# A gated delta rule kernel: state update over 128 rows, output products moved behind it, half-width masked copies, one gate projection for two heads

## What is computed

```
tri = tril(einsum('bhncd', k_beta, k) * decay, -1)
Tm = solve_triangular(eye + tri, eye)            # inverse of a 64x64 unit triangle per chunk
v_new = Tm @ v_beta ; k_cum = Tm @ (k_beta * exp(g))
def step(S, inp):                                # from chunk to chunk
    v_n = v_i - kc_i @ S
    out = (q_i * exp(g_i)) @ S + attn @ v_n
    S = S * exp(g_last) + (k_i * exp(g_last - g_i)).T @ v_n
```

## Time and profile before

| | |
|---|---|
| median of 3 runs | 3196.33 us (3190.98 to 3197.37) |
| the profiled execution | 3194.53 us, span 3192.8 us |
| granted TensorE clock, mean | 0.965 |
| TensorE busy | 2971.4 us, 93% of the span |
| VectorE busy | 2307.4 us, 72% |
| ScalarE, GpSimd busy | 1235.1 us, 1020.7 us |
| stage with the change | about 1000 to 2957 us of the span |

### The profile page before, as it was taken

One profiled execution on the slowest core, in us unless ns is written; L12 is line 12 of the kernel. 1 busy time (PEld: TensorE's weight loads), 2 busy tenths in 40 slices (PEclk: granted clock), 3 DMA queues, 4 the chain that ended last, 5 costly groups with the idle time before them and its releaser, 6 DMA issues. The chain is left out here.

```text
span 3192.8 us, 82005 instructions
## 1 busy us (share of the span) xinstructions
PE 2971.4 (93%) x33019; PEld 2051.3 (64%) x33019; DVE 2307.4 (72%) x5231; ACT 1235.1 (39%) x2975; POOL 1020.7 (32%) x1495
## 2 busy tenths in 40 slices
PE   6999999679997999999999999999999999999897
PEld 3444444246663777777777777777777777777565
DVE  4666677878874788688678678678678678676566
ACT  2433333323334344344344344344344344342354
POOL 3555455527772222222222222132132132121011
PEclk8999999789997999999999999999999999998899
DMA  2121111000001111001001001001001001000000
GB/s 83 36 58 31 32 31 34 22 1 1 1 1 47 32 41 32 22 19 32 22 18 32 21 19 32 19 21 32 19 21 32 19 22 32 18 18 2 4 25 27
DMA packets 94040, 80.43 MB, mean 25 GB/s; under 512 B 54992, under 2 KB 68320, under 8 KB 93664
## 3 DMA queue, kind: packets, MB, share of 16 engines
q1 hardware_dynamic: 93664, 75.18, 8.7%
HBM read 57.70 MB, written 4.85 MB: 20 GB/s over the span
## 5 line engine op out<-in xcount | busy, mean ns | idle before, releaser
L1828 PE MATMUL gd_bk<-gd_xT,gd_wh 128*128 128x512 f32 x768 | 397.3, 627 | 8.9 <-DVE gd_KE L1555 7.4
L480 DVE TENSOR_REDUCE at_nm<-at_ring 128x2 f32<-128x256 f32 (+3 forms) x256 | 199.2, 821 | 142.9 <-PE at_ring L623 142.9
L1537 DVE SCALAR_TENSOR_TENSOR gd_YK<-gd_bk,gd_cw,gd_YK 128x511 f32<-128x511 f32 (+2 forms) x384 | 283.1, 743 | 11.8 <-ACT gd_YK L1406 6.1
L1506 ACT COPY gd_ZS<-gd_bk 128x256 f32<-128x256 f32 x320 | 119.1, 372 | 318.3 <-PE gd_bk L2008 312.3
L2008 PE MATMUL gd_bk<-gd_L,gd_NT 64*64 64x64 f32 x5120 | 203.7, 223 | 26.5 <-DVE gd_L L1597 25.9
L2008 PEld LDWEIGHTS gd_bk<-gd_L,gd_NT 64*64 64x64 f32 x5120 | 169.2, 134 | 78.8 <-DVE gd_L L1597 40.2
L1595 DVE COPY_PREDICATED gd_U<-gd_mU,gd_bk 128x256 f32<-128x256 int32 x320 | 141.0, 442 | 105.5 <-PE gd_bk L2030 75.1
L1493 ACT COPY gd_O<-gd_bk 64x128 f32<-64x128 f32 x448 | 108.5, 259 | 274.8 <-PE gd_bk L1966 273.9
L2025 PE MATMUL gd_bk<-gd_U,gd_ZS 64*64 64x64 f32 x5120 | 207.6, 220 | 0.1
L302 POOL TENSOR_TENSOR at_PT<-at_PT,at_dm 128x1024 f32<-128x1024 f32 (+3 forms) x128 | 197.8, 1545 | 10.6
L2025 PEld LDWEIGHTS gd_bk<-gd_U,gd_ZS 64*64 64x64 f32 x5120 | 174.6, 135 | 40.8 <-issue 37.1
(11 more groups left out here) (354 smaller groups left out, 6772.0 us busy)
## 6 DMA issues: line engine op xcount, KB each, us to landing
gd_wh<-in_L_attn_W_qkvz SPq DMA_DIRECT2D x64, 512.0 KB, 3.7
gd_gb<-gates SPq DMA_DIRECT2D x128, 64.0 KB, 3.3
X<-in_L_attn_x SPq DMA_DIRECT2D x8, 512.0 KB, 8.7
at_QT<-at_QS SPq DMA_DIRECT2D x128, 32.0 KB, 2.0
at_KT<-at_KS SPq DMA_DIRECT2D x128, 32.0 KB, 2.0
at_OC<-at_Ob SPq DMA_DIRECT2D x128, 32.0 KB, 2.0
at_RC<-inverse SPq DMA_DIRECT2D x128, 32.0 KB, 1.8
out_x<-X SPq DMA_DIRECT2D x8, 512.0 KB, 2.9
```

The costliest lines, as they stand in the source:

```text
L480: nc.vector.tensor_reduce(nm[v % 2][:, k, c0:c0 + HS + 1:HS], set_of(s, 2 + p)[:, :, 0:n], AX.X, ALU.max).then_inc(max_done, 1)
L1537: nc.vector.scalar_tensor_tensor(out[:, s:W], bank_[:, 0:W - s], cw[:, j, head(f, e), CONVK - 1 - s:CONVK - s], out[:, s:W], ALU.mult, ALU ...
L1828: ins = nc.tensor.matmul(out[:, :], wh[e][:, k, col * DK:(col + 1) * DK], xT[:, k, :], start=k == 0, stop=k == DC - 1)
```

## The change

Four edits, all in `delta_rule`:

1. The state update of the rounds 1 to 7 contracts over all 128 rows. `V2` becomes a tile with one 128-row copy per chunk in which the other chunk's 64 rows are zero (cleared once by 4 memsets), and KK is read over all rows. The update of round 0 still has 64 rows.
2. TensorE computes the output products (odd rounds) directly behind the state update, ahead of the late piece of the next pair. Behind the levels the new values of both heads come first, then the new keys of both.
3. The masked copies of the levels 1 to 5 touch only the 32 of each 64 columns that the mask can select. Source, mask and destination are read in runs of 2, 4, 8, 16 or 32 columns. The masks are built 256 wide. The level 0 copies keep their width.
4. The gate projection computes both heads at once: 2 matmuls of 256 columns for each of 4 row tiles in place of 4 of 128. The weights of both heads lie in one tile and come by one DMA, which waits for the queries of both heads.

```diff
-        mU = [sb(f"mU{l}", [P, CK], I32) for l in range(LEVELS)]
+        mU = [sb(f"mU{l}", [P, TPS, CK], I32) for l in range(LEVELS)]
...
+        def side(tile, l, bit):
+            return tile[:, :, :].rearrange("p t (b s n) -> p (t b) s n", s=2, n=1 << l)[:, :, bit, :]
...
+        def bank_side(b_, half, l, bit):
+            return b_[:, half * TPS * CK:(half + 1) * TPS * CK].rearrange("p (b s n) -> p b s n", s=2, n=1 << l)[:, :, bit, :]
...
-        V2, O = [sb(f"V2{e}", [P, TPS, DK]) for e in E2], [sb(f"O{e}", [P, TPS, DK]) for e in E2]
+        V2, O = [sb(f"V2{e}", [P, 2, CPT, DK]) for e in E2], [sb(f"O{e}", [P, TPS, DK]) for e in E2]
...
                 def level(f, e, l):
                     dve.wait_ge(y_mm[e], f * (LEVELS - 1) + l)
-                    last = nc.vector.copy_predicated(U[e][:, :, :], wide(mU[l]), chunks(A_[e], 1))
+                    last = nc.vector.copy_predicated(side(U[e], l, 1), side(mU[l], l, 1), bank_side(A_[e], 1, l, 1))
                     if l < LEVELS - 1:
-                        last = nc.vector.copy_predicated(L[e][:, :, :], wide(mL[l]), chunks(A_[e], 0))
+                        last = nc.vector.copy_predicated(side(L[e], l, 0), side(mL[l], l, 0), bank_side(A_[e], 0, l, 0))
...
-                def gate_in(f, e, i):
-                    ge(pe, kc_done[e], f)
-                    for t in (2 * i, 2 * i + 1):
-                        for k in range(DC):
-                            last = nc.tensor.matmul(F1[e][:, t * P:(t + 1) * P], xT[:, k, t * P:(t + 1) * P], wh[e][:, k, 3 * DK:4 * DK],
-                                                    start=k == 0, stop=k == DC - 1)
-                    if i == 1:
-                        last.then_inc(zp_mm[e], 1)
+                def gate_in(f, t):
+                    i = t // 2
+                    ge(pe, kc_done[i], f)
+                    for k in range(DC):
+                        last = nc.tensor.matmul(F1[i][:, t % 2 * 2 * DK:(t % 2 + 1) * 2 * DK].rearrange("p (e n) -> p e n", e=2),
+                                                xT[:, k, t * P:(t + 1) * P], wh[:, k, :, 3 * DK:4 * DK], start=k == 0, stop=k == DC - 1)
+                    if t % 2 == 1:
+                        last.then_inc(zp_mm[i], 1)
...
-                                    moving = V2[e][rows(c), t, :]
-                                nc.tensor.matmul(A_[e][:, DK:2 * DK], KK[e][q % 2][rows(c), t, :], moving, start=True, stop=True).then_inc(ds_mm[e], 1)
-                        if has(f):
-                            front_late(f, n)
+                                    fixed, moving = KK[e][q % 2][:, t, :], V2[e][:, t % 2, c, :]
+                                nc.tensor.matmul(A_[e][:, DK:2 * DK], fixed, moving, start=True, stop=True).then_inc(ds_mm[e], 1)
...
                                 last.then_inc(oi_mm[e], 1)
+                        if has(f):
+                            front_late(f, n)
...
                             last.then_inc(vk_mm[e], 1)
+                        for e in E2:
                             pe.wait_ge(at_done[e], f + 1)
```

More of the change, by code:

```diff
@@ L971, in delta_rule @@
         m1, m2 = sb("m1", [P, CK], I32), sb("m2", [P, CK], I32)
-        mU = [sb(f"mU{l}", [P, CK], I32) for l in range(LEVELS)]
-        mL = [sb(f"mL{l}", [P, CK], I32) for l in range(LEVELS - 1)]
+        mU = [sb(f"mU{l}", [P, TPS, CK], I32) for l in range(LEVELS)]
+        mL = [sb(f"mL{l}", [P, TPS, CK], I32) for l in range(LEVELS - 1)]
         xT = sb("xT", [P, DC, W])
@@ L1175, in delta_rule @@
         kT, vT = [sb(f"kT{e}", [P, W]) for e in E2], [sb(f"vT{e}", [P, W]) for e in E2]
-        zz = [[sb(f"zz{e}{i}", [P, TPS, DK]) for i in range(2)] for e in E2]
+        zz = [sb(f"zz{i}", [P, 2, TPS, DK]) for i in range(2)]
         KK = [[sb(f"KK{e}{i}", [P, TPS, DK]) for i in range(2)] for e in E2]
@@ L1279, in _ @@
                 for f in range(PAIRS):
[L1280 to L1285, removed]
+                    if f > 0:
+                        h = head(f, 0)
+                        for e in E2:
+                            sp.wait_ge(qp_mm[e], f)
+                        sp.dma_start(wh[:, :, :, :].rearrange("p c e n -> p c (e n)"), Wq4[:, :, h * 4 * DK:(h + 2) * 4 * DK]).then_inc(w_in, 16)
                     if has(f + 1):
@@ L1312, in gate_weights @@
                 def gate_weights(f):
+                    for i in range(2):
+                        pool.wait_ge(z_silu[i], f + 1)
                     for e in E2:
-                        pool.wait_ge(z_silu[e], f + 1)
-                        nc.gpsimd.tensor_tensor(zz[e][f % 2][:, :, :], zz[e][f % 2][:, :, :],
+                        nc.gpsimd.tensor_tensor(zz[f % 2][:, e, :, :], zz[f % 2][:, e, :, :],
                                                 nw_row[:, :].unsqueeze(1).broadcast_to([P, TPS, DK]), ALU.mult).then_inc(zw_done[e], 1)
@@ L1732, in _ @@
                 nc.vector.tensor_copy(xT[:, 1, :], B_[1][:, :]).then_inc(xt_dve, 1)
+                for e in E2:
+                    for c in range(CPT):
+                        last = nc.vector.memset(V2[e][rows(1 - c), :, c, :], 0.0)
+                last.then_inc(v2_clear, 1)
                 for q in range(-1, PAIRS):
@@ L1826, in project @@
                 def project(out, e, col, k, done):
-                    ins = nc.tensor.matmul(out[:, :], wh[e][:, k, col * DK:(col + 1) * DK], xT[:, k, :], start=k == 0, stop=k == DC - 1)
+                    ins = nc.tensor.matmul(out[:, :], wh[:, k, e, col * DK:(col + 1) * DK], xT[:, k, :], start=k == 0, stop=k == DC - 1)
                     if k == DC - 1:
@@ L1976, in _ @@
                                     pe.wait_ge(kc_done[e], q + 1)
-                                    moving = VV[e][rows(c), t, :]
+                                    fixed, moving = KK[e][q % 2][rows(c), t, :], VV[e][rows(c), t, :]
                                 else:
@@ L1995, in _ @@
                                 for c in range(CPT):
-                                    source = VV if t == 0 and c == 0 else V2
-                                    last = nc.tensor.matmul(B_[e][rows(c), 0:DK], AT[e][q % 2][rows(c), t, :], source[e][rows(c), t, :],
+                                    moving = VV[e][rows(c), t, :] if t == 0 and c == 0 else V2[e][rows(c), t % 2, c, :]
+                                    last = nc.tensor.matmul(B_[e][rows(c), 0:DK], AT[e][q % 2][rows(c), t, :], moving,
                                                             start=True, stop=True)
                                 last.then_inc(oi_mm[e], 1)
+                        if has(f):
+                            front_late(f, n)
                     for l in range(1, LEVELS):
```

47 lines of the change are left out of this document (25 added, 22 removed).

## The result

The changed kernel takes 3081.27 us, the median of 4 runs (3073.21 to 3083.79), beside 3193.65 us for the kernel before (4 runs, 3189.51 to 3197.37). The ratio is 0.9644, with a 95% interval of 0.9620 to 0.9668: 112 us less. Forecast were 3071 us and 124 less.

The account below looks back on a forecast made before the run. TensorE's nearly gap-free list, busy 93% of the span, was taken as the bound. Terms 2.6 + 1.0 + 0.3 + 0.1 = 4.0 us per pair, times 31 pairs = 124, gave 3071 us, range 3036 to 3112.

Parts of the forecast that it names:

- A change of the array's shape costs 0.19 us: TensorE's state update: four passes end 0.64 us behind the gate instead of 0.45 when the array's rows change.
- the third rival: State update: its drain stays because the shape is not the cause; 2.5 us per pair gained, 3117 us, 4% chance.
- the side-by-side rule: State update: full height gives up small-row matmuls running side by side, losing 1.6 us per pair; 3120 us, 1% chance.
- Rounds 2.6 us per pair: Rounds 1 to 7: wider update and new order save 2.6 us per pair, about 0.8 of it waits.
- VectorE is late next: Round 5: two key norms and KK stand ahead of V, so TensorE again waits about 0.4 us for V.
- 1.0 us per pair: Levels: half-width copies save 0.3 to 0.45 us in each of three levels, 1.0 us per pair.
- I expect no price: Half-width masked copies on VectorE: reading in runs with gaps costs nothing extra, so a copy takes 309 ns instead of 442.
- copies at low levels are longer than at high ones: Level copies: a sign that the prediction is wrong; it expected about 310 ns at level 1 as at level 5.
- 0.3 us behind the levels: Behind the levels: two fewer changes of the array's shape at 0.15 us each save 0.3 us per pair.
- Gate, -0.1: Gate projection: 16 passes of 256 columns replace 32 of 128, changing TensorE's time by -0.1 us per pair.
- The edges cancel: Stage's prologue, first and last pair: wider masks cost 2.2 us at most, half hidden; the first pair gains 1.3 us.
- Copies don't shorten: Half-width level copies: a rival in which runs of few columns cost what they save; 3102 us, 12% chance.

Follow-up runs that it names:

- the first two experiments: The kernel before with only the 128-row state update, 3174.39 us; the kernel before with only the new order of output products, values and keys, 3123.33 us.
- packed masks: The changed kernel with the masks of level 1 packed without gaps, data still reached in runs of 2 columns: 3083.16 us, ratio 0.9658.
- level 0: The changed kernel with the masked copies of level 0 at half width too, every second column: 3082.42 us, ratio 0.9648.
- KK behind V: The changed kernel with KK of head 1 written behind V of round 5 on VectorE, no longer ahead of it: 3074.14 us, ratio 0.9625.
- the four with statistics moved: The changed kernel with statistics in round 0, 3066.42 us; cumulatively KK behind V, 3067.89; head 0's triangle product and first tap later, 3076.37; head 1's triangle product behind S, 3065.48.

## Why the forecast was right, and by how much it was off

*"A change of the array's shape costs 0.19 us"*: right, 0.64 against 0.45 in every round of the changed kernel where no wait is in it, and TensorE's list for a pair has 30 changes. With the wider update the drain is gone and no pass is longer; the third rival ("the update's drain stays") and the side-by-side rule are out. Two small slips cancel: 9 x 0.19 + 0.12 is 1.83 and not 1.87, and the change at the transposes, which stands in round 2, costs 0.15 and not 0.12 (they end 0.59 behind a 64-row update and 0.44 behind a 128-row one). By that rule of the Trainium skill (TensorE: Matmul & The Clock Gate, Part 3) the update would have lost 1.6 us per pair; the four passes still end 0.45 apart, as both heads' updates had used the same rows before.

*"Rounds 2.6 us per pair", of it 0.8 waits, plus 0.1 for the gate*: 2.58 together, worked out as how much earlier in the tenth pair the update of round 7 ends (27.04 us after the pair's start before, 24.46 now). The forecast of both was 2.7; the 0.12 between them were not traced, but for 0.07 in round 1, where the update ends at 0.52 and not at 0.45. The step behind it, that the order brings VectorE forward, is shown by the first two experiments: without it the wider update brings 0.53 us.

*"VectorE is late next", about 0.4 us in round 5*: 0.41 in plain pairs. In the pairs with statistics it is 2.02 us beyond 0.45, where before it was 1.94 beyond 0.64; I had read one kind of pair only. That changed little in the sum, but it hid what could be had next.

*"1.0 us per pair" in three levels*: 0.74. This is the term that was mis-sized, and *"I expect no price"* for runs is the step that failed. In the tenth pair TensorE gains 0.06 us between the levels 1 and 2, 0.39 between 2 and 3, nothing at level 4 and 0.28 at level 5. One row had shown an operation on every second column at the length of a dense one of as many columns, and I took that for all; but 128 columns in short runs take what 256 dense ones take. The copies ahead of level 2 did not shorten (only their distance did, from 0.33 to 0.25). Of the 12 us that the forecast is off, 0.26 x 31 = 8 come from there and 0.12 x 31 = 4 from the rounds and the gate. It also makes two of the signatures wrong: level 1 at 443 and 483 ns and not 310, the wait for L at 20.1 and not 15. And one of the forecast's own signs of being wrong came true, "copies at low levels are longer than at high ones". So for edit 3 the mechanism was wrong at one level of five, and the time came close because the copies of level 1 matter at one place only, 0.26 of the 4.0 us.

*"0.3 us behind the levels"*: 0.29. *Gate, -0.1*: 0.11 of busy time, and alone nothing in the time.

*"The edges cancel"*: about so. The last pair, which has no other work, was 5.7 us shorter in the profiled run (from its first update to the end of the stage 45.8 us before, 40.1 now), where I had said "no drain is saved". But the granted clock is 0.5 for 30.7 us of that stretch in the trace of before and for 10.2 in that of after. The run with the packed masks, whose rounds are those of the changed kernel, has 30.7 and 45.7 us; the run with the half-width copies alone, whose rounds are those of before, has 10.2 and 40.4 us. So the clock differs from one execution to the next, and at the same clock the last pair gained 0.3 us.

Of the rivals none came true as a whole. *Copies don't shorten* (3102) is what level 1 did, one level of five.

## What to carry to other kernels

What a shorter list of the busiest engine brings is settled by the engine that it waits for: the wider update took 1.3 to 1.7 us of drains out of a pair and brought 0.53 us alone and 0.77 with the order (2.58 less the order's 1.71 and 0.1 for the gate), as V, and behind it the scales, were late next. A wait that one reordering removes comes back at the next consumer of the same engine; work moved into an engine's idle time (the statistics into round 0) makes it go. And where a strided form has several run lengths, its shortest needs a row or a bound of its own.

## What the runs showed of the hardware

A masked copy on VectorE from PSUM, means of 64 copies or more: 128x256 dense 436 to 442 ns, 128x128 in runs of 4 to 32 columns 287 to 301 ns, in runs of 2 columns 443 (U) and 483 ns (L), in runs of 1 column 467 ns (L) and, from SBUF, 445 ns (U). The distance between starts of two such copies falls all the same, from 0.33 us to 0.25 (runs of 2) and 0.21 (longer).

A stand of TensorE in an otherwise dense stretch can be followed by 3.4 us at 1.2 GHz (6.8 in one place). Counted over the seven pairs with statistics of one profiled run each, by how much later the update of round 5 ended than without a wait:

```
stand us   kernel                          falls of the clock, of 7
2.3        wider update alone              7
2.0        changed; packed masks; level 0  3, 3, 3
2.0        full-width copies put back      1
1.9        before; copies; gate            4, 4, 2
1.6        order alone                     3
1.4        KK behind V                     0
0.4 or 0   the four with statistics moved  0, 0, 0, 0
```

At equal stands the count is not the same: every fall in these pairs came with a stand of 1.6 us or more, and a stand of that length did not always bring one.
